# Long attention of a decoder: weighing in bursts of two groups every fourth tick, with 12 exponential buffers, remainders and jobs moved beside the bursts

## The chip, the cores and the metric

The kernel runs on one core of one Trainium2 chip, as one launch. The metric is the time of the whole launch on the device, in microseconds; lower is better. Work inside the core is split over engines with queues of their own: TensorE (PE), whose weight loads are listed apart as PEld, VectorE (DVE), ScalarE (ACT), GpSimd (POOL) and SyncE (SP), which here issues transfers. They meet at semaphores alone.

## The reference

A decoder of four layers over 8 batches of 100 tokens with 128 features, with three different blocks in each layer. Eleven of the twelve blocks are untouched by the change. The one that is touched is the eleventh, cross attention of the tokens to a context of 1444 rows with 16 query heads of 8 features and 4 key heads:

```python
# B=8, query length 100, key length 1444, H=16, HK=4, HD=8, G=4
q = (query @ Wq).reshape(b, qlen, H, HD)
k = (key @ Wk).reshape(b, kvlen, HK, HD)
v = (value @ Wv).reshape(b, kvlen, HK, HD)
scores = einsum('bqkgd,bskd->bkgqs', q.reshape(b, qlen, HK, G, HD), k) / sqrt(HD)
attn = softmax(scores, axis=-1)
out = einsum('bkgqs,bskd->bqkgd', attn, v).reshape(b, qlen, H * HD)
return out @ Wo
```

The kernel computes it together with the twelfth block (a small network with binarised weights) in `attention_long`, the last stage of the launch.

## The kernel before

`attention_long` works through batches `b` and, in each, two pairs of heads `p`. A unit `u = 2*b + p` is one pair of heads of one batch. The softmax needs the largest score of each row first, so every score is computed twice. In the first pass `max_scores` (L770) multiplies 128 query rows by 361 keys and VectorE takes the negated maximum straight from PSUM (`maximum`, L521); the rows of the fourth part of the queries are few, and four products of another tile shape, "remainders" (L764, read by L516), take care of them. `combine` (VectorE), `split` (GpSimd), the job NT (`turn_maxima`, L780 and L782 on TensorE), `maxima` (the NB copy on ScalarE, L692) and `add_maxima` (GpSimd, L465) then bring the maxima as extra rows into the queries. In the second pass `score` (L793) computes 128 keys by 400 columns, ScalarE turns them to exponentials (`exps`, L679) into one of `EB` buffers of the tile `E`, and `weigh` (L810) multiplies them by the values into `pO`. A group is two key tiles; `weigh(u, g)` issues its four products, in float32, each in a column group of 32 of the array, so that the four run side by side. The profile has two records for each float32 product, thus eight for a group.

The order on each engine is written out by ticks `t`; a batch begins every `PER` = 26 ticks. A tick with offset `o = t - 26*b` holds on TensorE: two `max_scores`, alternating with two `score`s where a unit is in its second pass, then the jobs of the tick, then a weighing if `group_step(t)` names one. Unit `u` has its 12 score steps from tick `start(u)` on: `26*b + 20` for even units, 13 ticks later for odd ones. So of 26 ticks 24 have two scores each, and offsets 6 and 19 have none. In the kernel before a group is weighed at every second tick, from the third step after `start(u)` on, at offsets 23, 25, 1, 3, 5, 7 and 10, 12, 14, 16, 18, 20. Remainders take the place of `max_scores` at offsets 12 and 13 (`REM_AT`).

Five jobs go with a batch: NT twice, TM (`token_major`, eight small float32 products, L820), TURN (`turn`, L827) and PROJ (`project`, L831). Jobs and scores write to PSUM banks that `banks_in_turn` deals out from estimates in ticks: in the steady part there are three, each given to the item that asks when it has been free longest. A score holds its bank until its exponential has been taken, a job until its reader has read it, and `bank_read` makes TensorE wait for exactly that. From tick `start(15)` on five banks are dealt; from tick 208 (`DRAIN`), when there are no more `max_scores`, jobs have a bank of their own. The four banks `pM` of the first pass wait for VectorE.

ScalarE's order in a tick is: the tick's two exponentials, then `out_copied`, then `maxima` (one tick after NT) or `outT` (one tick after TURN). The first `score` of a unit waits for `add_maxima` of that unit.

Of the kernel before, what the change touches and what calls it, by code (L numbers as in the profile page):

```python
# [14 lines left out]
B, T, D = 8, 100, 128  # L15
# [6 lines left out]
NKT = KT_FULL + 1  # L22
# [213 lines left out]
def attention_long(nc, m, name, wo, out):  # L236
# [3 lines left out]
    PER = 26  # L240
    REM_AT = 12
    S_AT = 20
    NU = 2 * B
    EB = 8

    KEY0 = [CW * (k % 4) + 128 * (k // 4) for k in range(NKT)]
    NT0_AT, NT1_AT, TM_AT, TURN_AT, PROJ_AT = 16, 28, 48, 56, 60
    LAST = PER * (B - 1) + PROJ_AT + 1
    SIGNS_AT = (10, 15)
    DRAIN = PER * B  # L250
# [3 lines left out]
    with ExitStack() as ctx:  # L254
# [3 lines left out]
        QT = s.sb("QT", [128, 3, TOK], BF16)  # L258
        E = s.sb("E", [128, EB, NG * T])
        XQ = s.sb("XQ", [128, TOK])  # L260
# [45 lines left out]
        def start(u):  # L306
            return PER * (u // 2) + S_AT + 13 * (u % 2)

        def unit_step(t):

            for u in range(NU):
                if 0 <= t - start(u) < NKT:
                    return u, t - start(u)
            return None

        def group_step(t):

            for u in range(NU):
                r = t - start(u) - 3
                if 0 <= r < NKT and r % 2 == 0:  # L320
                    return u, r // 2
            return None

# [55 lines left out]
        def score_bank(n):  # L379
            return bank_of["score", n]  # L380

        def key_rows(ap, a):
            return ap[64 * a:64 * a + 64]

        with nc.Block() as block:
# [244 lines left out]
            def _(act):  # L630
# [40 lines left out]
                def exps(u, k):  # L671
                    for a in range(2):
                        n = 24 * u + 2 * k + a
                        act.wait_ge(s_s, n + 1)
                        if n >= EB:
                            v, kk = (n - EB) // 24, (n - EB) % 24 // 2
                            act.wait_ge(s_pv, 4 * (6 * v + kk // 2 + 1))
                        r = NW[k]
                        nc.scalar.activation(E[0:r, n % EB, :], score_bank(n)[0:r, 0:NG * T], ACT.Exp,  # L679
                                             scale=SCALE8).then_inc(s_e, 1)  # L680
# [44 lines left out]
            def _(pe):  # L725
                def bank_read(item):
                    holder = earlier_in_bank[item]
                    if holder is not None and holder[0] == "score":
                        pe.wait_ge(s_e, holder[1] + 1)
                    elif holder is not None:  # L730
                        pe.wait_ge(s_read, number[holder] + 1)
# [19 lines left out]
                def max_scores(n):  # L751
                    b, o = n // (2 * PER), n % (2 * PER)
                    if o == 0:
                        if b >= KB:
                            pe.wait_ge(s_ks, 32 * (b - KB + 1))
                        pe.wait_ge(s_qs, 32 * (b + 1))
                    if n >= 4:
                        pe.wait_ge(s_mr, n - 3)
                    if o // 2 in (REM_AT, REM_AT + 1):
                        if o == 2 * REM_AT:  # L760
                            pe.wait_ge(s_qr, b + 1)
                        c = o - 2 * REM_AT
                        for p in range(2):
                            nc.tensor.matmul(pM[32 * p:32 * p + 32, n % 4, 0:CW], QR[:, p, b, :],  # L764
                                             KS[:, b % KB, c, p, :], start=True, stop=True,
                                             skip_group_check=True).then_inc(s_m, 1)
                    else:
                        p, i = (0, o // 2) if o < 2 * REM_AT else (1, o // 2 - REM_AT - 2)
                        x, c, a = i // NC4, i % NC4, 1 - o % 2
                        nc.tensor.matmul(pM[:, n % 4, 0:CW], key_rows(QS, a)[:, b, p, 128 * x:128 * x + 128],  # L770
                                         key_rows(KS, a)[:, b % KB, c, p, :],
                                         start=True, stop=True).then_inc(s_m, 1)

                def turn_maxima(u):
                    pP = fill(("NT", u))
                    pe.wait_ge(s_mx, u + 1)
                    if u == 0:
                        pe.wait_ge(s_rs, 1)
                    for x in range(3):
                        nc.tensor.matmul(pP[:, 128 * x:128 * x + 128], MXP[:, u % 2, x, :], m.ident16[:, :],  # L780
                                         start=(x == 0), stop=True, skip_group_check=True)
                    nc.tensor.matmul(pP[:, 384:NG * T], MXP[0:64, u % 2, 3, :], RS[:, :], start=False, stop=True,  # L782
                                     skip_group_check=True).then_inc(s_fill, 1)

                def score(u, k, a):
                    b, p = u // 2, u % 2
                    n = 24 * u + 2 * k + a
                    if k == 0:
                        pe.wait_ge(s_add, u + 1)
                    bank_read(("score", n))  # L790
                    if n >= 24 * (NU - 1):
                        pe.wait_ge(s_mr, 2 * DRAIN)
                    nc.tensor.matmul(score_bank(n)[0:NW[k], 0:NG * T],  # L793
                                     key_rows(KS, a)[:, b % KB, k % 4, p, 128 * (k // 4):128 * (k // 4) + NW[k]],
                                     key_rows(QS, a)[:, b, p, :],
                                     start=True, stop=True).then_inc(s_s, 1)

                def weigh(u, g):
                    b, p = u // 2, u % 2
                    pe.wait_ge(s_e, 24 * u + 4 * g + 4)  # L800
                    if u == 0 and g == 0:
                        pe.wait_ge(s_ws, 2)
                    if g == 0 and p == 0 and b >= 1:
                        pe.wait_ge(s_oc, b)
                    for x in range(2):
                        k = 2 * g + x
                        for a in range(2):
                            n = 24 * u + 2 * k + a
                            r = 32 * (2 * x + a)
                            nc.tensor.matmul(pO[r:r + 32, 0:NG * T], V[0:NW[k], b, k, a, 16 * p:16 * p + 32],  # L810
                                             E[0:NW[k], n % EB, :], start=(p == 0 and g == 0),
                                             stop=(p == 1 and g == 5), skip_group_check=True).then_inc(s_pv, 1)
# [12 lines left out]
                def turn(b):  # L825
                    pP = fill(("TURN", b))
                    nc.tensor.transpose(pP[:, 144:144 + T], ON[:, :], m.ident[0:T, 0:T]).then_inc(s_fill, 1)  # L827
# [50 lines left out]

                for t in range(LAST + 1):
                    at_step = unit_step(t)  # L880
                    for a in range(2):
                        if t < PER * B:
                            max_scores(2 * t + a)
                        if at_step is not None:
                            score(*at_step, a)
                    for b in range(B):
                        o = t - PER * b
                        if o == NT0_AT:
                            turn_maxima(2 * b)
                        if o == NT1_AT:  # L890
                            turn_maxima(2 * b + 1)
                        if o == TM_AT:
                            token_major(b)
                        if o == TURN_AT:
                            turn(b)
                        if o == PROJ_AT:
                            project(b)
                    at_group = group_step(t)
                    if at_group is not None:
                        weigh(*at_group)  # L900
                    for i in range(2):
                        if t == SIGNS_AT[i]:
                            turn_signs(i)
                        if t == DRAIN + (16, 18)[i]:
                            turn_rows(i)
                    if t == start(NU - 1) + 13:
                        up(0)
                    if t == PER * (B - 1) + TM_AT + 2:
                        up(1)
                        down(0)  # L910
                    if t == PER * (B - 1) + TURN_AT:
                        up(2)
# [15 lines left out]
def attention_short(nc, m, name, wq, wk, wv, wo, spare, keys="self", bias=None, beside=None):  # L928
# [3 lines left out]
    KD = VH * HD  # L932
    EB = 4
    N = 2 * B
# [2903 lines left out]
def decoder(nc, a, out):  # L3838

    with ExitStack() as ctx:  # L3840
# [112 lines left out]
        if 10 in n:  # L3953
            attention_delta_rule(nc, m)
        held["L3a"].close()
        attention_long(nc, m, "L3x", w["x3o"][:, :], out)


# [197 lines left out]
```

## Time and profile before

| | us |
|---|---|
| median of 3 runs (1068.70, 1074.39, 1077.85) | 1074.39 |
| profiled execution | 1076.63 |
| its span from first to last instruction | 1074.8 |

The profiled execution is 2.2 us above the median, and 1.8 us of it lie outside the span. The long attention begins at about 800 us; its first pass starts at 809 us, its first score at 829 us, its last score at 1051.7 us, and the rest up to 1074.8 us is the end of the last batch and of the twelfth block. Views used below: the page, busy time by stretches, groups of instructions by line, waits, and the timeline. In the timeline a row is a run of equal instructions on an engine: start, time from the first start to the last end, engine, line, operation, output and inputs, shape, count, and in brackets the idle time before it with what ended it. The records of TensorE overlap: their length holds the way through the array too, so that the distance between starts, not the length, says how long the engine was taken.

### The profile page before, as it was taken

The numbers are of one execution on the slowest core, as the hardware profiler recorded it, in microseconds if no ns is written. First come the engines' busy times: TensorE is split into PE (matmuls) and PEld (weight loads), VectorE is DVE, ScalarE is ACT, GpSimd is POOL, SyncE is SP. The second block draws the span as 40 slices with busy tenths as digits, with TensorE's granted clock in tenths as the row PEclk, the third lists the DMA queues.
The fourth block names the chain that finished last, engine by engine and source line by source line (L and its number), as shares of the span: only waits on it lengthen the run. The fifth ranks groups of instructions, "written<-read, shape, count | busy, mean of one in ns | idle before, by whom it ended". The sixth has DMA issues, their size and how long they took to land. (4 is left out here: it accounts for less than half of the span.)

```text
span 1074.8 us, 18594 instructions
## 1 busy us (share of the span) xinstructions
PE 907.2 (84%) x6319; PEld 555.0 (52%) x6328; DVE 740.8 (69%) x2034; ACT 583.3 (54%) x1772; POOL 241.7 (22%) x357
## 2 busy tenths in 40 slices
PE   7998999999797372599679799795768999999997
PEld 4447999998464130345453386492662233333333
DVE  7658777877574798475776555514658888888853
ACT  5885777777323100343535344641443777777784
POOL 5013555554200122233030000341401111111110
PEclk8999999999999685699766999996885999999999
DMA  9610000000003600000001001650212101111000
GB/s 234 156 25 2 2 1 2 2 2 1 1 1 45 78 1 15 16 1 2 0 26 31 1 1 56 180 152 17 43 27 64 25 14 18 27 28 22 2 2 16
DMA packets 76186, 35.85 MB, mean 33 GB/s; under 512 B 35236, under 2 KB 74571, under 8 KB 76092
## 3 DMA queue, kind: packets, MB, share of 16 engines
q1 hardware_dynamic: 73724, 33.61, 13.9%
q8 instruction: 51, 0.84, 0.3%
q0 software_dynamic: 896, 0.63, 0.2%
q10 hardware_dynamic: 1472, 0.41, 0.2%
q14 instruction: 43, 0.35, 0.1%
HBM read 24.42 MB, written 11.05 MB: 33 GB/s over the span
## 5 line engine op out<-in xcount | busy, mean ns | idle before, releaser
L679 ACT ACTIVATE L3x_E<-L3x_pS 128x400 f32<-128x400 f32 (+1 forms) x374 | 163.9, 509 | 48.2 <-PE L3x_pS L793 46.7
L521 DVE TENSOR_REDUCE L3x_NMP<-L3x_pM 128x1 f32<-128x361 f32 x384 | 176.0, 524 | 18.5 <-PE L3x_pM L770 17.5
L793 PE MATMUL L3x_pS<-ctx_tm 64*128 64x400 bf16 (+1 forms) x374 | 102.8, 347 | 5.7 <-ACT L3x_E L679 2.6
L1911 ACT ACTIVATE L0x_E<-L0x_E,ctx_r 128x100 f32<-128x100 f32 x288 | 105.1, 369 | 0.5 <-DVE L0x_E L1791 0.5
L770 PE MATMUL L3x_pM<-ctx_tm 64*128 64x361 bf16 x384 | 97.3, 336 | 3.3 <-DVE L3x_NMP L521 2.4
L810 PE MATMUL L3x_pO<-L3x_E,CT 128*32 128x400 f32 (+1 forms) x768 | 84.8, 514 | 0.6 <-ACT L3x_E L679 0.4
L770 PEld LDWEIGHTS L3x_pM<-ctx_tm 64*128 64x128 bf16 x384 | 29.3, 100 | 79.3 <-DVE L3x_NMP L521 62.6
L1720 POOL TENSOR_TENSOR L0x_E<-L0x_E,L0x_RZ 128x1200 f32<-128x1200 f32 x24 | 52.6, 2192 | 72.4 <-DVE L0x_RZ L1816 72.4
L2037 PE MATMUL L0x_pU<-ctx_tm,L0x_E 128*100 128x129 f32 x576 | 67.8, 273 | 1.1 <-POOL L0x_E L1720 1.1
L2025 PE MATMUL L0x_pS<-L0x_QS,CT 128*128 128x100 f32 x576 | 68.4, 275 | 0.0
L2025 PEld LDWEIGHTS L0x_pS<-L0x_QS,CT 128*128 128x128 f32 x576 | 66.2, 192 | 0.4 <-ACT L0x_QS L1903 0.4
L2037 PEld LDWEIGHTS L0x_pU<-ctx_tm,L0x_E 128*100 128x100 f32 x576 | 64.7, 166 | 2.3 <-POOL L0x_E L1720 1.9
L1911 ACT ACTIVATION_READ_ACCUMULATOR L0x_E<-L0x_E,ctx_r 128x1 f32 x288 | 54.9, 191 | 0.0
L793 PEld LDWEIGHTS L3x_pS<-ctx_tm 64*128 64x128 bf16 (+1 forms) x374 | 30.9, 104 | 46.3 <-ACT L3x_E L679 39.7
L2563 PE MATMUL L1a_pA<-CT,ident 128*128 128x512 f32 (+1 forms) x48 | 24.8, 680 | 27.3 <-DVE CT L2432 27.3
L2416 POOL TENSOR_TENSOR L1a_W<-CT,L1a_KV 128x1280 f32<-128x1280 f32 x5 | 16.1, 3220 | 125.7 <-ACT L1a_KV L2513 87.7
L1784 DVE TENSOR_REDUCE L0x_mx<-L0x_pS 128x4 f32<-128x400 f32 x72 | 40.8, 569 | 2.7 <-PE L0x_pS L2025 1.0
L1791 DVE TENSOR_TENSOR L0x_E<-L0x_pS,L0x_mx 128x400 f32<-128x400 f32 x72 | 38.8, 566 | 0.1
L455 POOL TENSOR_SCALAR L3x_MXP<-L3x_nmx 128x8 bf16<-128x8 f32 x16 | 4.2, 261 | 144.6 <-DVE L3x_nmx L534 144.6
L3053 POOL DMA_INDIRECT slots_in<-L2f_XE,L2f_slot_index x8 | 8.8, 1097 | 119.1 <-issue 119.1
L137 ACT ACTIVATE root<-veps 100x8 f32<-100x8 f32 (+1 forms) x11 | 2.3, 210 | 60.9 <-DVE veps L120 37.7
L2563 PEld LDWEIGHTS L1a_pA<-CT,ident 128*128 128x128 f32 x48 | 11.3, 243 | 40.7 <-issue 34.1
(727 smaller groups left out, 2134.4 us busy)
## 6 DMA issues: line engine op xcount, KB each, us to landing
ctx_tm<-in_ctx SPq DMA_DIRECT2D x8, 704.0 KB
ctx_tm<-key_terms SPq DMA_DIRECT2D x16, 270.8 KB, 4.2
key_terms<-ctx_tm SPq DMA_DIRECT2D x42, 90.2 KB
ctx_tm<-in_L_ffn_wi SPq DMA_DIRECT2D x4, 512.0 KB, 7.5
ctx_tm<-in_L_ffn_wo SPq DMA_DIRECT2D x4, 512.0 KB, 7.8
ctx_tm<-query_terms SPq DMA_DIRECT2D x16, 75.0 KB, 3.3
slots_in<-L2a_zeros SPq DMA_DIRECT2D x8, 129.0 KB
L2f_XS<-slots_in SPq DMA_DIRECT2D x4, 258.0 KB, 3.1
```

The lines of the kernel that those rows point to most:

```text
L521: nc.vector.tensor_reduce(NMP[:, p, i // NC4, a, i % NC4:i % NC4 + 1], v, AX.X, ALU.max, negate=True).then_inc(s_mr, 1)
L679: nc.scalar.activation(E[0:r, n % EB, :], score_bank(n)[0:r, 0:NG * T], ACT.Exp, scale=SCALE8).then_inc(s_e, 1)
L770: nc.tensor.matmul(pM[:, n % 4, 0:CW], key_rows(QS, a)[:, b, p, 128 * x:128 * x + 128], key_rows(KS, a)[:, b % KB, c, p, :], start=True, s ...
L793: nc.tensor.matmul(score_bank(n)[0:NW[k], 0:NG * T], key_rows(KS, a)[:, b % KB, k % 4, p, 128 * (k // 4):128 * (k // 4) + NW[k]], key_rows ...
L810: nc.tensor.matmul(pO[r:r + 32, 0:NG * T], V[0:NW[k], b, k, a, 16 * p:16 * p + 32], E[0:NW[k], n % EB, :], start=(p == 0 and g == 0), stop ...
L1720: nc.gpsimd.tensor_tensor(E[:, n % 3, :, :], E[:, n % 3, :, :], RZ[:, n % 2, :].unsqueeze(2).broadcast_to((128, 12, T)), ALU.mult).then_in ...
L1784: nc.vector.tensor_reduce(mx[:, n % 2, 4 * c:4 * c + 4], pS[:, g % SB, 0:4 * T].rearrange("p (k t) -> p k t", t=T), AX.X, ALU.max).then_in ...
L1791: nc.vector.tensor_tensor(E[:, n % 3, 4 * c:4 * c + 4, :], pS[:, g % SB, 0:4 * T].rearrange("p (k t) -> p k t", t=T), mx[:, n % 2, 4 * c:4 ...
L1911: last = nc.scalar.activation(E[:, n % 3, k, :], E[:, n % 3, k, :], ACT.Exp, scale=m.ctx_r[:, n % B, k:k + 1], accum_out=Z[:, n % 2, k:k + 1])
L2025: last = nc.tensor.matmul(pS[:, g % SB, k * T:(k + 1) * T], m.CT[:, n % B, c:c + 128], QS[:, n % 2, :], start=True, stop=True)
L2037: last = nc.tensor.matmul(pU[0:T, 0:D + 1], E[:, n % 3, k, :], m.ctx_tm[:, n % B, k, :], start=(k == 0), stop=(k == NKT - 1))
L2563: last = nc.tensor.matmul(pC[n % 2][:, c:c + x], m.ident[:, :], P[:, n % 2, c:c + x], start=(i == 0), stop=True, skip_group_check=True)
```

## The change

The buffers for exponentials grow from 8 to 12. `group_step` names every fourth tick, from the fifth step after `start(u)` on, and two groups are weighed there one after the other: bursts at offsets 25, 3, 7 and 12, 16, 20, with sixteen records each. At offset 12 the two remainders are issued behind the tick's scores, just ahead of the burst, and at offset 13 ahead of the scores, just behind the burst. NT1 moves from offset 2 to 3, TM from 22 to 25, TURN from 4 to 1, and PROJ from 8 to 7; NT0 stays at 16. The readers of the jobs on the other engines move along, each one tick behind its job, because they are placed by the same constants. The products, their number and their shapes are the same.

```diff
@@ -241,10 +241,10 @@
     REM_AT = 12
     S_AT = 20
     NU = 2 * B
-    EB = 8
+    EB = 12
 
     KEY0 = [CW * (k % 4) + 128 * (k // 4) for k in range(NKT)]
-    NT0_AT, NT1_AT, TM_AT, TURN_AT, PROJ_AT = 16, 28, 48, 56, 60
+    NT0_AT, NT1_AT, TM_AT, TURN_AT, PROJ_AT = 16, 29, 51, 53, 59
@@ -316,8 +316,8 @@
         def group_step(t):
 
             for u in range(NU):
-                r = t - start(u) - 3
-                if 0 <= r < NKT and r % 2 == 0:
+                r = t - start(u) - 5
+                if 0 <= r < NKT and r % 4 == 0:
                     return u, r // 2
             return None
 
@@ -878,11 +878,18 @@
 
                 for t in range(LAST + 1):
                     at_step = unit_step(t)
+                    remainder = t % PER - REM_AT if t < PER * B else None
+                    if remainder == 1:
+                        max_scores(2 * t)
+                        max_scores(2 * t + 1)
                     for a in range(2):
-                        if t < PER * B:
+                        if t < PER * B and remainder not in (0, 1):
                             max_scores(2 * t + a)
                         if at_step is not None:
                             score(*at_step, a)
+                    if remainder == 0:
+                        max_scores(2 * t)
+                        max_scores(2 * t + 1)
                     for b in range(B):
                         o = t - PER * b
                         if o == NT0_AT:
@@ -897,7 +904,9 @@
                             project(b)
                     at_group = group_step(t)
                     if at_group is not None:
-                        weigh(*at_group)
+                        u, g = at_group
+                        weigh(u, g)
+                        weigh(u, g + 1)
```

## Rows read from the trace of the kernel before

**Rows 1.** The page: granted TensorE clock in 40 slices of the span, in tenths.
```profile
PEclk8999999999999685699766999996885999999999
```

**Rows 2.** Busy time of each engine (instructions) in one period of 26 ticks.
```profile
894.60:923.40 28.80, 27.82 (x223) 9.25 (x219) 25.48 (x64) 22.23 (x53) 4.05 (x12) 1.00 0.16 26
```

**Rows 3.** Groups by line in that period: busy us, mean ns, idle before.
```profile
L521 DVE TENSOR_REDUCE L3x_NMP<-L3x_pM 128x1 f32<-128x361 f32 x50 | 23.1, 525 | 2.6 <-PE L3x_pM L770 2.5
L679 ACT ACTIVATE L3x_E<-L3x_pS 128x400 f32<-128x400 f32 (+1 forms) x49 | 21.6, 506 | 6.4 <-PE L3x_pS L793 6.2
...
L810 PE MATMUL L3x_pO<-L3x_E,CT 128*32 128x400 f32 (+1 forms) x100 | 11.1, 511 | 0.0
```

**Rows 4.** Waits in that period: who for whom, us, times, longest.
```profile
ACT L3x_E L679 <- PE L3x_pS L793: 6.2, 12, 0.9
PEld L3x_pS L793 <- ACT L3x_E L679: 5.0, 14, 0.7
```

**Rows 5.** Timeline of two ticks without a job, offsets 24 and 25.
```profile
919.58 0.49 PE L793 MATMUL L3x_pS<-ctx_tm 64*128 64x400 bf16 x2
...
919.98 1.69 ACT L679 ACTIVATE L3x_E<-L3x_pS 128x400 f32<-128x400 f32 x4 [0.34 <-PE L3x_pS L793]
...
920.53 0.34 PE L793 MATMUL L3x_pS<-ctx_tm 64*128 64x400 bf16 x1
...
920.81 0.88 PE L810 MATMUL L3x_pO<-L3x_E,CT 128*32 128x400 f32 x8
...
921.62 0.32 PE L770 MATMUL L3x_pM<-ctx_tm 64*128 64x361 bf16 x1
...
922.01 1.69 ACT L679 ACTIVATE L3x_E<-L3x_pS 128x400 f32<-128x400 f32 x4 [0.34 <-PE L3x_pS L793]
```

**Rows 6.** Timeline: weighings at offsets 3, 7, 12, 16, 20, then 3; a remainder behind one.
```profile
896.51 0.88 PE L810 MATMUL L3x_pO<-L3x_E,CT 128*32 128x400 f32 x8
...
900.37 0.88 PE L810 MATMUL L3x_pO<-L3x_E,CT 105*32 105x400 f32 x8
...
906.05 0.88 PE L810 MATMUL L3x_pO<-L3x_E,CT 128*32 128x400 f32 x8
906.75 0.33 PE L764 MATMUL L3x_pM<-ctx_tm 128*32 128x361 bf16 x2
...
910.80 0.88 PE L810 MATMUL L3x_pO<-L3x_E,CT 128*32 128x400 f32 x8
...
914.80 0.88 PE L810 MATMUL L3x_pO<-L3x_E,CT 105*32 105x400 f32 x8
...
925.31 0.88 PE L810 MATMUL L3x_pO<-L3x_E,CT 128*32 128x400 f32 x8
```

**Rows 7.** Timeline behind the weighing of offset 7, with PROJ: two banks for scores.
```profile
901.61 0.46 PE L831 MATMUL L3x_pS<-w_x3o,L3x_OT 128*100 128x128 f32 x2
...
902.14 0.34 PE L793 MATMUL L3x_pS<-ctx_tm 64*128 64x400 bf16 x1
...
903.07 0.34 PE L793 MATMUL L3x_pS<-ctx_tm 64*128 64x400 bf16 x1
```

**Rows 8.** Timeline from NT0 (offset 16) to the first score of the unit.
```profile
910.43 0.33 PE L780 MATMUL L3x_pS<-ident,L3x_MXP 128*128 128x128 bf16 x3
...
912.80 0.49 ACT L692 CAST L3x_NB<-L3x_pS 128x400 bf16<-128x400 f32 x1
...
913.37 0.94 POOL L465 TENSOR_TENSOR ctx_tm<-ctx_tm,L3x_NB 128x400 bf16<-128x400 bf16 x1 [3.34 <-ACT L3x_NB L692]
...
914.37 0.43 PE L793 MATMUL L3x_pS<-ctx_tm 64*128 64x400 bf16 x2
```

**Rows 9.** Timeline behind the weighing of offset 20: exponentials, TM, the next product.
```profile
916.21 1.70 ACT L679 ACTIVATE L3x_E<-L3x_pS 128x400 f32<-128x400 f32 x4
...
917.22 1.19 PE L820 MATMUL L3x_pS<-L3x_selP,L3x_OC 128*100 128x144 f32 x8
918.34 0.33 PE L770 MATMUL L3x_pM<-ctx_tm 64*128 64x361 bf16 x1
```

## The prediction

> **What bounds the kernel now.** I read the page first: from 845 us on TensorE has its full clock, all last slices are nines [rows 1], so a stretch of the long attention can be reckoned in fixed durations. Then the busy time of one period of 26 ticks [rows 2]: of 28.80 us TensorE is busy 27.82, VectorE 25.48, ScalarE 22.23. TensorE looks like the bound, but its records overlap and hold waiting inside the array, so I went on to the waits. ScalarE waits for scores 6.2 us of a period, and TensorE's score loads wait for exponentials 5.0 us [rows 4]. Each waits for the other: a loop, not an engine, sets the pace. The timeline of two ticks shows the loop [rows 5]. Take the first product behind a weighing as time 0 (919.58). The first exponential starts at 0.40. The first three scores have a bank at once; the fourth (920.53, at 0.95) has none before the first exponential is done, 0.56 after that one's start. The weighing starts 0.27 behind that score (920.81), and the next row product 0.81 later (921.62): 0.95 + 0.27 + 0.81 = 2.03 us. ScalarE has run dry meanwhile, 0.34 us. Four exponentials take 1.69 us with one of 0.51 [rows 3, 5], so they follow each other at (1.69 - 0.51) / 3 = 0.39.
>
> **The rule for a stretch.** With three banks score k (k of 4 or more) starts at 0.95 + 0.39 (k - 4). Where a job holds one bank there are two: scores start at 0, 0.17, 0.95, 1.35, 1.90, 2.30, 2.85, 3.25. Rows 7 bear this out: behind the weighing that starts at 900.37 (0 is at 901.18), the third and fifth scores come at 0.96 and 1.89 [rows 6, 7]. VectorE needs 23.1 / 50 = 0.46 a maximum [rows 3]. If its first starts as late as ScalarE's, four banks hold the eighth product until the fourth maximum is taken, 0.40 + 4 x 0.46, about 2.3; that counts only where a stretch has few scores.
>
> **What a burst costs.** Eight records last 0.88 and one 0.51 on average, so the second four start about 0.36 behind the first [rows 3, 5]. Two groups in one burst need two more such passes: 0.81 + 2 x 0.36 = 1.53 us. Bounds: 0.70 more, the distance at which a remainder follows a weighing [rows 6], or a second full 0.81. The saving is real but small. A remainder has the weighing's tile shape and follows at 0.70, a row product at 0.81 [rows 5, 6]: leaving the shape costs 0.11. Two scores take 0.49 and one 0.34, so a score keeps its rows 0.16; entering costs 0.27 less that, 0.11. A pair is worth 0.2 us. Six weighings and about three pairs round the remainders go away in a period: 1.8 us, if nothing else waited.
>
> The Trainium skill, TensorEngine Tiling (Array Packing), Key Properties, says that changing the tiling mode drains the engine; the two prices above agree, and by that rule alone the change would gain (the rival below). Its section PSUM Bottleneck says that tiling hastens TensorE but not the emptying of PSUM, which can become the limit; the three banks of this trace behave so.
>
> What the saving is set against: during 0.27 + 1.53 us of each burst, and 0.40 more until a new score reaches ScalarE, only the scores that three banks hold can be turned, 3 x 0.39 = 1.2 us. Behind it the banks come free one by one at ScalarE's pace, and TensorE cannot work ahead. EB = 12 does not lift this: it holds exponentials, not scores, and it is just what the longer distance to the burst needs. The price of EB itself is nothing.
>
> **The six stretches**, each from the start of one burst to the next; before is read from the starts in [rows 5, 6], after is the 1.53 of the burst, the last score by the rule, 0.27, and what the jobs add.
> - Offsets 25 to 3, before 4.50. Eight scores, but the planner deals one bank to TM (held by estimate for 2.8 ticks from 25), to TURN at 1 and to NT1 at 3, so scores have two: the eighth at 3.25. NT1 then adds 0.25, a change of shape from a score, and 0.37 until the burst [rows 6, 8]: 3.87 + 1.53 = 5.40.
> - 3 to 7, before 3.86. NT1 now lies just ahead of a burst, and its copy NB on ScalarE stands behind the exponentials of offset 4, which come after the burst. Rows 8 show the same at offset 16: from the end of the weighing (911.61) to the first score of the unit (914.37) 2.76 us pass, through two exponentials, NB (0.49) and the addition on POOL (0.94). The unit's first score, the fifth of this stretch, cannot start before 2.76; by the banks it could at 1.9. Before, NB ran under the weighing and this wait wasn't there at offset 7. With the sixth at 2.92 and PROJ (0.46 [rows 7] and a change of shape), about 0.6 until the burst: 3.50 + 1.53 = 5.03.
> - 7 to 12, before 5.68. Ten scores, one bank dealt to PROJ for the first: the tenth at 3.47; two remainders, 0.27 to the first as to a weighing and 0.15 each: 4.04 + 1.53 = 5.57. Residual and statistics on VectorE lie under the burst.
> - 12 to 16, before 4.75. Two remainders first, 0.30, then eight scores, the last at 2.81. NT0 waits for the bank of the sixth exponential, 0.30 + 0.40 + 5 x 0.39 + 0.56, about 3.20; 0.37: 3.57 + 1.53 = 5.10.
> - 16 to 20, before 4.00. Six scores, the fifth at 2.76 by the addition: 2.87 + 0.32 + 1.53 = 4.72. Before, a weighing lay in this very wait and cost nothing. Now it lies in the bursts.
> - 20 to 25, before 6.01. Ten scores, the first exponential 0.2 late by the copy of `pO` (916.21 is 0.60 behind 915.61 [rows 6, 9]): the tenth at 3.50; TM waits for the bank of the eighth exponential until 3.94, its eight products take 0.94 up to the burst (1.12 to a row product [rows 9]): 4.88 + 1.53 = 6.41. VectorE's normalising lies under the burst.
>
> Sum: before 28.80, after 32.23, +3.4 us. From the burst of tick 25 to that of tick 207 there are seven periods: +24.0.
>
> Ends: up to tick 215 the drain has the same two bad stretches without maxima, +0.7 and +1.9. Behind it five banks hold 1.9 us of exponentials against a silence of 1.80 + 0.40: +0.5 for two bursts. Near the end TURN stands ahead of two pieces of the last block that lay under VectorE's normalising: +0.5. The first ticks at half clock I leave at zero. Total +27.6. The profiled execution would go from 1076.6 to 1104; the median lies 2.2 below it, so **1102 us** (1074.4 + 27.6).
>
> **The rivals.**
> 1. The burst starves ScalarE, but the additions and the two-bank stretches are hidden: three-bank times throughout with VectorE's hold at 2.3 give 4.7, 4.4, 5.4, 5.1, 4.1 and 6.2, in all 29.9, +1.1 a period, with the ends about +10: 1084. For it: estimates of the planner are not waits. Against it: rows 7 and 8 show both waits as they stand. Chance 0.14.
> 2. The other side: the switches of shape set the pace, and the bank waits are only where TensorE happens to stand. It decides if scores can be issued less than 0.39 apart on average behind a burst. Then 9 pairs x 0.2 = 1.8 us a period go, 7.5 periods: 1061. For it: TensorE's 27.82 of 28.80 busy [rows 2]. Against it: the fourth score of every stretch waits for an exponential [rows 4, 5]. Chance 0.08.
> 3. Gains and losses cancel, 1070 to 1080: chance 0.06, for sums of many small terms. A second group that costs 0.81 rather than 0.72 adds 48 x 0.09 = 4; a clock that falls because TensorE waits more would add beyond 1112, 0.02.
>
> **How the numbers follow.** The forecast has 0.70, its own range 1092 (additions hidden in half of the cases, passes at 0.34) to 1112 (second group at 0.81, further job waits of 0.6 a period). Rival 1 carries the low end to 1080. Range 1080 to 1113. Taking 1% as what can be told from no change (1063.6 to 1085.1): slower 0.80, the forecast and part of rival 1; same 0.12; faster 0.08.
>
> **What would show it.** In the changed kernel: sixteen L810 records in about 1.6 us; a period of 32.2 us against 28.8; ScalarE's idle before L679 from 6.4 to about 9 us a period; in the stretch behind offset 3 a first score of the unit that waits for L465, 2.8 behind the burst; scores behind the burst of offset 25 in pairs 0.95 apart. A period under 28.8 with scores 0.17 apart would make the prediction wrong at its root; a period near 30 makes only the job terms wrong.

## The result and the profile after

The changed kernel takes 1116.74 us (median of four runs, 1110.68 to 1124.89); the kernel before ran beside it at 1072.26 us. The ratio is 1.0412, with a 95% interval of 1.037 to 1.0455: 4% slower, 44.5 us. The forecast was 1102, slower by 27.6, with a range to 1113. The direction was right, the size was not.

The profiled execution is the slowest of the four, 1124.89 us, with a span of 1123.1; that is 48.3 us more than the span before. Its mean granted clock is 0.893, that of the other three 0.902, so what this trace says of the clock is more than a middle execution has. The page of the changed kernel gives the first hint. This is the granted clock of TensorE in 40 slices, to be laid beside [rows 1]:

```profile
PEclk8998999999996875998888999969769888879999
```

Before, the last nine slices are all nines. Here four eights and a seven stand in a row in the middle of the long attention. The next fence is the timeline of the changed kernel, weighings alone: start and length of four bursts of sixteen records.

```profile
1017.02 1.55 PE L810 MATMUL L3x_pO<-L3x_E,CT 128*32 128x400 f32 x16
...
1022.08 1.55 PE L810 MATMUL L3x_pO<-L3x_E,CT 105*32 105x400 f32 x16
...
1032.70 1.55 PE L810 MATMUL L3x_pO<-L3x_E,CT 128*32 128x400 f32 x16
...
1037.36 1.55 PE L810 MATMUL L3x_pO<-L3x_E,CT 105*32 105x400 f32 x16
```

They stand at offsets 3, 7, 16 and 20; the burst of offset 12 starts at 1027.34. A burst of two groups lasts 1.55 us from first start to last end, against 0.88 for one group [rows 6]. From 1022.08 to 1032.70, over offsets 7 to 16, 10.62 us pass where 10.43 passed before [rows 6]; the two stretches on either side, 5.06 and 4.66, took 3.86 and 4.00. From earlier in the timeline of the changed kernel come the burst of offset 20, the job TM, the burst of offset 25 and two rows of the scores behind it:

```profile
894.60 1.55 PE L810 MATMUL L3x_pO<-L3x_E,CT 105*32 105x400 f32 x16
900.07 1.20 PE L820 MATMUL L3x_pS<-L3x_selP,L3x_OC 128*100 128x144 f32 x8
901.20 1.55 PE L810 MATMUL L3x_pO<-L3x_E,CT 128*32 128x400 f32 x16
...
902.68 0.49 PE L793 MATMUL L3x_pS<-ctx_tm 64*128 64x400 bf16 x2
...
903.63 0.34 PE L793 MATMUL L3x_pS<-ctx_tm 64*128 64x400 bf16 x1 [0.31 <-ACT L3x_E L679]
```

Offsets 20 to 25 take 6.60 (6.01 before). Offsets 25 to 3 take 5.42 (937.06 to 942.48; 4.50 before). Put together from such stretches, a period at full clock is 32.37 us against 28.80. What seven periods take in this trace, 245.6 us from the burst of tick 25 (832.34) to that of tick 207 (1077.94), is more than seven periods at full clock. These would be about 31.23 + 6 x 32.37 = 225.4: the first of the seven is shorter than the others, 31.23 in a kernel with the same order of products that has it whole at full clock (the one with maxima over 64 columns, below). The rest, 20.2 us, is clock.

The busy times of each engine in short stretches of the changed kernel (us, busy and instructions for PE, PEld, DVE, ACT, POOL, then the granted clock, the share of the DMA engines and GB/s) show what one such place looks like:

```profile
872.50:875.90 3.40, 2.47 (x20) 0.98 (x16) 3.02 (x7) 2.32 (x6) 1.19 (x2) 1.00 0.00 0
875.90:879.30 3.40, 3.40 (x20) 0.77 (x21) 0.79 (x3) 0.65 (x2) 0.00 (x0) 0.50 0.00 0
...
927.10:930.50 3.40, 2.48 (x20) 0.83 (x21) 3.40 (x8) 2.75 (x7) 0.94 (x1) 1.00 0.27 74
930.50:933.90 3.40, 3.40 (x23) 0.89 (x15) 1.51 (x5) 1.89 (x6) 0.00 (x0) 0.51 1.01 134
```

In the first row of each pair TensorE is busy 2.5 of 3.4 us and has the full 2.4 GHz; in the row behind it it is busy throughout and has 1.2 GHz. Each slow row holds a burst or a part of one. Both quiet rows lie in a stretch in which the first score of a unit waits for the addition on GpSimd.

Such rows stand ahead of only half of the falls. Of the twelve half-clock stretches of this trace between 846 and 1048 us, one of 10.2 us and eleven of 3.4, six come behind 3.4 us with 2.47 to 2.52 busy; the other six come behind 2.94 to 3.09, in stretches without a wait for the addition. And TensorE can be less busy than in these and keep its clock. The same view at such a fall, and at a stretch with less work and no fall:

```profile
903.20:906.60 3.40, 3.05 (x17) 1.18 (x16) 3.40 (x8) 3.29 (x9) 0.00 (x0) 1.00 0.00 0
906.60:910.00 3.40, 3.40 (x21) 0.93 (x21) 0.20 (x2) 0.24 (x1) 0.00 (x0) 0.51 0.03 5
...
893.00:896.40 3.40, 2.80 (x27) 0.91 (x26) 2.40 (x6) 1.91 (x6) 0.94 (x1) 1.00 0.63 126
896.40:899.80 3.40, 3.06 (x20) 0.85 (x14) 3.35 (x8) 3.40 (x10) 0.00 (x0) 1.00 0.73 82
```

The timeline of the changed kernel for the first quiet row, at 872.50:

```profile
871.03 1.55 PE L810 MATMUL L3x_pO<-L3x_E,CT 128*32 128x400 f32 x16
872.52 0.32 PE L770 MATMUL L3x_pM<-ctx_tm 64*128 64x361 bf16 x1
872.52 0.49 PE L793 MATMUL L3x_pS<-ctx_tm 64*105 64x400 bf16 x2
...
872.92 0.90 ACT L679 ACTIVATE L3x_E<-L3x_pS 105x400 f32<-105x400 f32 x2 [1.67 <-PE L3x_pS L793]
873.48 0.37 PE L793 MATMUL L3x_pS<-ctx_tm 64*105 64x400 bf16 x1 [0.32 <-ACT L3x_E L679]
...
873.71 0.50 ACT L692 CAST L3x_NB<-L3x_pS 128x400 bf16<-128x400 f32 x1
...
874.28 0.94 POOL L465 TENSOR_TENSOR ctx_tm<-ctx_tm,L3x_NB 128x400 bf16<-128x400 bf16 x1 [7.09 <-ACT L3x_NB L692]
...
875.28 0.43 PE L793 MATMUL L3x_pS<-ctx_tm 64*128 64x400 bf16 x2 [0.60 <-POOL ctx_tm L465]
...
876.20 0.89 PE L810 MATMUL L3x_pO<-L3x_E,CT 105*32 105x400 f32 x4
```

The row product (L770) is 1.49 behind the start of the burst. ScalarE had been idle 1.67 us when its first exponential came. The first score of the odd unit (875.28) comes 2.76 behind the end of the burst (872.52, where the next product starts), exactly as at offset 16 before [rows 8], and TensorE had waited 0.60 for L465.

### The profile page after: what moved, and what is told of

Same layout as the page of the kernel before. It is cut to its first block and busy times, and to the rows that moved or that the text cites. A ratio compares the mean times of both kernels' runs of the same rounds, so it can differ in the third digit from the quotient of the medians.

```text
span 1123.1 us, 18599 instructions
## 1 busy us (share of the span) xinstructions
PE 933.7 (83%) x6328; PEld 569.9 (51%) x6328; DVE 735.8 (66%) x2034; ACT 578.4 (52%) x1772; POOL 244.2 (22%) x357
## 5 line engine op out<-in xcount | busy, mean ns | idle before, releaser
L679 ACT ACTIVATE L3x_E<-L3x_pS 128x400 f32<-128x400 f32 (+1 forms) x374 | 160.3, 524 | 96.1 <-PE L3x_pS L793 95.2
L793 PE MATMUL L3x_pS<-ctx_tm 64*128 64x400 bf16 (+1 forms) x374 | 115.1, 366 | 22.8 <-ACT L3x_E L679 12.6
L770 PE MATMUL L3x_pM<-ctx_tm 64*128 64x361 bf16 x384 | 109.5, 349 | 2.5 <-DVE L3x_NMP L521 2.0
L810 PE MATMUL L3x_pO<-L3x_E,CT 128*32 128x400 f32 (+1 forms) x768 | 93.5, 598 | 0.1
L770 PEld LDWEIGHTS L3x_pM<-ctx_tm 64*128 64x128 bf16 x384 | 34.9, 105 | 56.4 <-DVE L3x_NMP L521 27.8
L2425 POOL TENSOR_TENSOR L1a_W<-CT,L1a_KV 128x1280 f32<-128x1280 f32 x5 | 18.7, 3737 | 124.6 <-ACT L1a_KV L2522 88.4
L1793 DVE TENSOR_REDUCE L0x_mx<-L0x_pS 128x4 f32<-128x400 f32 x72 | 40.8, 568 | 2.9 <-PE L0x_pS L2034 1.2
L810 PEld LDWEIGHTS L3x_pO<-L3x_E,CT 128*32 128x32 f32 (+1 forms) x768 | 25.2, 122 | 32.2 <-issue 21.8
L465 POOL TENSOR_TENSOR ctx_tm<-ctx_tm,L3x_NB 128x400 bf16<-128x400 bf16 x16 | 15.0, 938 | 91.1 <-ACT L3x_NB L692 91.1
```

Of the source, the lines that this page charges most:

```text
L793: nc.tensor.matmul(score_bank(n)[0:NW[k], 0:NG * T], key_rows(KS, a)[:, b % KB, k % 4, p, 128 * (k // 4):128 * (k // 4) + NW[k]], key_rows ...
L1793: nc.vector.tensor_reduce(mx[:, n % 2, 4 * c:4 * c + 4], pS[:, g % SB, 0:4 * T].rearrange("p (k t) -> p k t", t=T), AX.X, ALU.max).then_in ...
```

## The experiments

Theory A, of the prediction: a burst outlasts what three score banks hold, and the moved jobs put new waits into the loop of TensorE and ScalarE. Theory B, formed from the trace after: on top of that TensorE then has too little to do, its clock falls to the lower level for some microseconds, and bursts run at half speed (the busy time of single rows alone cannot show it, as the rows above say; the runs have to). Rivals: the jobs alone carry the loss; the banks are not what counts; the clock falls for the long float32 bursts themselves.

**Bursts alone.** The kernel before with this and nothing else:

```diff
-    EB = 8
+    EB = 12
-                r = t - start(u) - 3
-                if 0 <= r < NKT and r % 2 == 0:
+                r = t - start(u) - 5
+                if 0 <= r < NKT and r % 4 == 0:
-                        weigh(*at_group)
+                        u, g = at_group
+                        weigh(u, g)
+                        weigh(u, g + 1)
```

> The bursts of two groups every fourth tick and the 12 buffers alone; the jobs and the remainders stay where they are in the kernel before. Theory of the prediction (three score banks run dry under a burst of 1.5 us, whatever stands beside it): a period of about 31.3 us at full clock against 28.8, thus 1090 to 1095, and more if the TensorE clock falls as it does in the changed kernel. Rival (the loss is in the moved jobs, NT1's copy above all, and the burst itself is harmless): a period within 0.5 us of 28.8, 1070 to 1077.

Measured: 1090.75 us, ratio 1.014 (1.0114 to 1.0166). The period is 30.72 us, read from the starts of bursts 26 ticks apart (894.71, 925.42, 956.14). The clock is whole, as the busy times of one period show:

```profile
925.40:956.10 30.70, 28.54 (x220) 10.37 (x219) 25.38 (x63) 21.87 (x53) 4.04 (x11) 1.00 0.15 24
```

Theory A holds in kind, 1.9 us a period where 2.5 were expected, although this kernel has the 12 buffers. The rival of the harmless burst falls.

**Moved jobs and remainders alone.** The changed kernel with `EB = 8`, offset 3 and `r % 2` in `group_step`, and one `weigh` for a call.

> The moved jobs and remainders alone, with single groups at every second tick and 8 buffers. Theory: the shape changes round the remainders go (0.6 us a period), NT1 ahead of a weighing makes the unit's first score wait for the addition on GpSimd (0.2 to 0.5 a period): 1069 to 1076, and the clock stays whole. Rival (the moved jobs carry the loss): 1085 or more.

Measured: 1093.38 us, ratio 1.0167 (1.0136 to 1.0199), a period of 30.50. This was a miss, and the rival named with it was right: they cost 1.70 us a period, nearly as much as the bursts. The timeline shows one reason. TM stands right ahead of the weighing now, so ScalarE gets nothing for the length of both, and is idle 1.64 us; TM at its old place left it idle 0.83.

```profile
892.12 1.20 PE L820 MATMUL L3x_pS<-L3x_selP,L3x_OC 128*100 128x144 f32 x8
...
893.25 0.88 PE L810 MATMUL L3x_pO<-L3x_E,CT 128*32 128x400 f32 x8
...
894.46 1.84 ACT L679 ACTIVATE L3x_E<-L3x_pS 128x400 f32<-128x400 f32 x4 [1.64 <-PE L3x_pS L793]
...
895.01 0.34 PE L793 MATMUL L3x_pS<-ctx_tm 64*128 64x400 bf16 x1 [0.31 <-ACT L3x_E L679]
```

The last row is the third score behind the weighing, 0.95 behind its first: two banks, because the third is dealt to TM, then to TURN.

**Which part of these.** Three kernels, each the one before with one part. Remainders:

> The kernel before with only the new places of the remainders: behind the scores of offset 12, ahead of those of offset 13, next to the single weighing of offset 12. The run with moved jobs and remainders had a period of 30.50 against 28.80, with 0.65 less from offset 7 to 12 and 0.42 more from 12 to 16. Theory (the remainders give back shape changes, the loss there is the jobs' alone): a period of 28.2 to 28.8, 1070 to 1075. Rival (the remainders ahead of offset 13 delay scores and maxima and carry a part of the 1.7): a period of 29.0 or more, 1077 or more.

Measured: 1073.36 us, ratio 0.9983 (0.9963 to 1.0003). The period is 28.98, 0.18 more. That lies between what the theory (up to 28.8) and the rival (29.0 or more) expected. From offset 7 to 12 0.25 us are saved, from 12 to 16 0.42 are lost. The time cannot be told from that before.

TM alone, `TM_AT` 48 to 51:

> The kernel before with TM alone moved, from offset 22 to 25 (TURN, NT1 and PROJ as before). The moved jobs and remainders cost 1.7 us a period together, the remainders 0.2 of it. Theory (TM and the weighing right behind it are one silence of two microseconds for ScalarE, and TM's bank is dealt away for the ticks behind it): 0.8 to 1.2 a period, 29.6 to 30.0, 1081 to 1086. Rival (TM only changes places with as much waiting, the loss is with NT1, TURN and PROJ): 29.1 or less, up to 1077.

Measured: 1078.78 us, ratio 1.0062 (1.0033 to 1.009), a period of 29.55, 0.75 more: both just under the theory's range, the time above the rival's. Of it 0.35 lie between offsets 20 and 25 (3.04 + 3.33 against 3.97 + 2.04) and 0.40 in the next stretch.

NT1, TURN and PROJ, `NT1_AT` 28 to 29, `TURN_AT` 56 to 53, `PROJ_AT` 60 to 59:

> The kernel before with NT1, TURN and PROJ at their new places and TM and the remainders where they were. Theory (TM carries the most): 0.2 to 0.6 a period more, 29.0 to 29.4, 1074 to 1080. Rival (NT1's late copy and the shortened chain carry the loss): 29.8 or more, 1082 or more.

Measured: 1080.54 us, ratio 1.0082 (1.0053 to 1.0112), a period of 29.75, 0.95 more, above the theory's 0.2 to 0.6 and next to the rival's 29.8. So TM does not carry the most. The three parts add to 1.88 where the kernel with all of them has 1.70. With the bursts: 1.92 + 1.70 = 3.62, and the changed kernel at full clock has 3.57 more than before. The losses simply add.

**One job back.** The changed kernel with `NT1_AT = 28`.

> The changed kernel with NT1 one tick earlier (28, as before), so that its copy on ScalarE stands ahead of the burst of offset 3 and runs beneath it. Theory: the first score of the odd unit no longer waits for the addition on GpSimd; the stretch from offset 3 to 7 goes from 5.06 to 4.2 to 4.4 us, 0.7 to 0.9 a period, about 6 us less than the changed kernel, give or take what the clock does. Rival (that wait lies beside VectorE's hold on the last maxima and is worth nothing): no difference to the changed kernel beyond its spread.

Measured: 1109.32 us, ratio 1.0324 (1.0288 to 1.036). The stretch from offset 3 to 7 is 4.50 in place of 5.06; the one ahead of it takes 5.61 instead of 5.42, so at full clock a period is 31.98, 0.38 less. That is 2.7 us over seven periods. The ratios differ by 0.0088, 9.4 us, with intervals that just part; the other 7 may lie with the clock, as this trace has four half-clock stretches of 3.4 us in its periods in place of twelve. It is not shown that the earlier NT1 is the reason: the number changes from kernel to kernel without it too (the next run has five with the order of the changed kernel). The wait is real, and about half of what it was thought to be worth.

**A fourth bank for scores.** First the ground, the changed kernel with maxima over 64 of the 361 columns, which leaves a part of the maxima out:

```diff
-                    v = pM[:, n % 4, 0:CW]
+                    v = pM[:, n % 4, 0:64]
```

> The changed kernel with each maximum taken over 64 of the 361 columns of its product (a part of the maxima is left out), so that VectorE cannot hold the banks of the first pass; the ground for the next run. Both theories: little change, 32.0 to 32.4 a period where the clock is whole, as the banks of the scores and not VectorE set the pace; if VectorE's maxima set it, 31 or less.

Measured: 1106.84 us (two runs, ratio 1.0304, 1.0255 to 1.0353), and 32.36 a period at full clock, the same as with full maxima, although VectorE falls to 12.08 us busy of 32.40. VectorE does not set the pace of the changed kernel. The median is all the same 9.9 us lower. This trace has five half-clock stretches of 3.4 us in its first three periods and then four whole periods without one, with the same products in the same order: when the clock falls is not settled by the order alone. The waits of one of the whole periods, to be laid beside [rows 4], show the loop at the new pace:

```profile
PEld L3x_pS L793 <- ACT L3x_E L679: 10.5, 28, 0.7
ACT L3x_E L679 <- PE L3x_pS L793: 9.8, 7, 2.3
```

TensorE's score loads wait 10.5 us of a period for exponentials where they waited 5.0. Then the bank (shortened):

```diff
-        shared = [pS[:, 0, :], pS[:, 1, :], pS[:, 2, :], pM[:, 1, :], pM[:, 2, :]]
+        shared = [pS[:, 0, :], pS[:, 1, :], pS[:, 2, :], pM[:, 3, :], pM[:, 1, :], pM[:, 2, :]]
-                usable = 5 if t >= start(NU - 1) else 3
+                usable = (0, 1, 2, 4, 5) if t >= start(NU - 1) else (0, 1, 2) if t >= DRAIN else (0, 1, 2, 3)
-                    if n >= 4:
-                        pe.wait_ge(s_mr, n - 3)
+                    if n >= 3:
+                        pe.wait_ge(s_mr, n - 2)
```

and `n % 3` in place of `n % 4` for the first pass's banks.

> As the run with maxima over 64 columns, but with three banks for the first pass and four instead of three dealt to scores and jobs. Theory (three banks hold too few scores for a burst): the last score ahead of a burst comes 0.39 earlier where no job holds a bank and 0.74 earlier where one does, nothing where the addition on GpSimd is awaited: 1.9 us a period less than the run with three banks, 30.2 to 30.6 at full clock, 14 us or more in all. Rival (banks are only where TensorE happens to stand, the order of products sets the pace): within 3 us of the run with three banks.

Measured: 1088.44 us (two runs), 18.4 less, and a period of 30.62, 1.74 less; 1.9 were expected. Seven periods of it make 12.2 of the 18.4. The busy times of one period, first with three banks for scores, then with four:

```profile
963.60:996.00 32.40, 28.72 (x224) 10.43 (x223) 12.08 (x62) 21.53 (x52) 4.09 (x12) 1.00 0.10 18
```

```profile
950.80:981.40 30.60, 27.65 (x220) 10.58 (x219) 11.87 (x62) 21.23 (x53) 4.03 (x12) 1.00 0.10 20
```

The same products in the same order, one bank more for scores: the banks are what a burst runs out of. The clock falls here too, three times in the seven periods, for 3.4 us each. The stretches that wait for the addition kept their 5.06 and 4.67.

**The same for the kernel before**, with all of the work:

> The kernel before with three banks for the first pass and four dealt to scores and jobs, all of the work done. With maxima over few columns a fourth bank was worth 1.74 us a period of the changed kernel. Theory: single weighings leave silences of 0.27 + 0.81 + 0.43, 1.5 us, which three banks of maxima (1.3 us of VectorE's work) just do not cover, so that VectorE, 25.5 of 28.8 busy, takes 0.2 more per weighing while scores gain: 28.3 to 29.0 a period, 1068 to 1076. Rival (score banks are what bounds the kernel before too, and VectorE has room): 28.0 or less, 1066 or less.

Measured: 1072.14 us, ratio 0.9995 (0.9971 to 1.0018), a period of 28.50, 0.30 less. What the scores gain the maxima lose: the stretches from offset 5 to 7 and 18 to 20 go from 1.39 and 1.53 to 2.12, three with a job from 2.47 to 2.08, and in a period the loads of the row products wait 11.2 us for maxima where they waited 6.7. No version that beats the kernel before came out of this.

**The clock, held.** The changed kernel with more streaming where TensorE waits for ScalarE:

```diff
+                        t = n // 2
+                        if t > start(0) and unit_step(t) is not None and group_step(t - 1) is None:
+                            nc.tensor.matmul(pM[:, n % 4, 0:CW], key_rows(QS, a)[:, b, p, 128 * x:128 * x + 128],
+                                             key_rows(KS, a)[:, b % KB, c, p, :], start=True, stop=True)
```

> The changed kernel with each product of the first pass issued twice into the same bank (the second overwrites the first with the same numbers) in ticks with scores that are not the first behind a burst: more streaming on TensorE where it waits for ScalarE. Theory (the half-clock stretches of the changed kernel come from TensorE having too little to do behind and between bursts): no half-clock stretch between 860 us and the end of the second pass, a period of 32.4 to 33 us throughout, 1100 to 1106. Rival (the clock falls for the long float32 bursts themselves, or by chance of the run): half-clock stretches stay, 1116 or more.

Measured: 1108.01 us, ratio 1.0304 (1.0276 to 1.0333), below the interval of the changed kernel (1.037 to 1.0455) with 34 products more in a period, and above the 1100 to 1106 that were expected. The busy times of two periods:

```profile
894.40:927.20 32.80, 30.68 (x258) 13.23 (x261) 25.44 (x63) 21.53 (x52) 4.07 (x11) 1.00 0.14 23
927.20:960.00 32.80, 30.68 (x258) 13.22 (x261) 25.43 (x63) 21.53 (x52) 4.07 (x11) 1.00 0.14 23
```

Every period from 861 to 1058 us is 32.78, at full clock. Behind them, in the drain, where there are no products of the first pass left to double, one half-clock stretch of 10.2 us comes at 1068 us: there the expectation missed. The extra products cost 0.41 a period, the clock gave back more. The mean granted clock of the whole launch agrees in every execution and not only in the profiled one: 0.912 to 0.915 in the four of this run, 0.893 to 0.902 in the four of the changed kernel. The same bursts are in it, so they do not make the clock fall by themselves.

**The clock, lost without bursts.** The kernel before with two banks for scores and jobs (`usable = 5 if t >= start(NU - 1) else 2`), one look:

> The kernel before with two instead of three banks dealt to scores and jobs. By the rule for two banks a pair of ticks without a job takes 2.43 instead of 2.03 us, and where a job holds a bank scores come 0.95 apart: a period of 33 to 36 us. If the clock falls because TensorE has little to do (and not for long float32 bursts, of which this kernel has none), half-clock stretches come in the second pass here too; if it falls for the bursts, none.

Measured: 1139.28 us in a single run, periods of 37.4 to 40.8 behind the first, longer than the 33 to 36 expected: where a job holds one of two banks only one is left. Two pairs of stretches:

```profile
892.90:896.30 3.40, 2.52 (x24) 0.70 (x16) 2.04 (x4) 2.15 (x5) 0.77 (x1) 1.00 0.00 0
896.30:899.70 3.40, 3.40 (x24) 0.62 (x18) 1.86 (x4) 1.08 (x4) 0.17 (x1) 0.50 0.83 152
930.40:933.80 3.40, 2.52 (x20) 0.70 (x16) 1.99 (x4) 2.02 (x5) 0.64 (x1) 1.00 0.02 5
933.80:937.20 3.40, 3.40 (x24) 0.54 (x18) 1.91 (x5) 1.16 (x3) 0.31 (x1) 0.50 0.79 150
```

The same picture as in the changed kernel, without one burst of two groups: 2.5 us busy of 3.4, then half clock. But this trace has the same rows without a fall behind them:

```profile
909.90:913.30 3.40, 2.47 (x24) 0.85 (x20) 1.95 (x4) 2.29 (x5) 0.00 (x0) 1.00 0.02 5
913.30:916.70 3.40, 2.51 (x21) 0.92 (x20) 1.95 (x4) 2.04 (x5) 1.19 (x2) 1.00 0.00 0
```

So theory B stands as far as this: more waits can bring half-clock stretches, without bursts of two groups too, and in the changed kernel products put into the waits took them out of the seven periods. Which wait tips the clock, and when, no run here settles.

## Why the prediction was right in direction and wrong in size

**The loop and the bank rule: right.** At full clock the six stretches came out as follows.

| offsets | before | forecast | measured |
|---|---|---|---|
| 25 to 3 | 4.50 | 5.40 | 5.42 |
| 3 to 7 | 3.86 | 5.03 | 5.06 |
| 7 to 12 | 5.68 | 5.57 | 5.26 |
| 12 to 16 | 4.75 | 5.10 | 5.36 |
| 16 to 20 | 4.00 | 4.72 | 4.67 |
| 20 to 25 | 6.01 | 6.41 | 6.60 |
| period | 28.80 | 32.23 | 32.37 |

Seven periods cost 225.4 - 200.7 = 24.7 us more (before, 835.31 to 1036.01, its first one shorter too), the sum had 24.0. The experiment with the fourth bank confirms the rule itself, 1.74 against 1.9.

**The price of a burst: right within 0.05.** 1.49 from its start to the next row product, 1.53 forecast. The other marks named there are seen too: sixteen records in 1.55 us, the unit's first score 2.76 behind the burst, scores 0.95 apart behind the burst of offset 25 (902.68 and 903.63). ScalarE's idle time before its exponentials was forecast at about 9 us a period; in the whole period of the kernel with maxima over 64 columns, of the same length, the waits for scores alone are 9.8.

**Offsets 7 to 16: two errors that cancel.** Forecast 10.67, measured 10.62, and that is luck: the first part is 0.31 shorter and the second 0.26 longer than forecast. The start of the burst of offset 12 came earlier than reckoned, because part of it did not wait for the remainders (below), and the end did not.

**The rivals.** Rival 1, additions and two-bank stretches hidden, is refuted by the stretches 3 to 7 and 25 to 3. Rival 2, shape changes set the pace, is refuted by the periods of the bursts alone and of the fourth bank; where shape changes alone were saved, round the remainders, the run cannot be told from before. Rival 3, gains and losses cancel, is refuted by the time.

**The step that failed: the clock.** The prediction took the full clock of [rows 1] for given in the changed kernel too ("a stretch of the long attention can be reckoned in fixed durations"), and gave a falling clock a chance of 0.02, although it had itself worked out that TensorE would wait more. What the runs showed in its place is a clock that falls to 1.2 GHz for 3.4 us and more at twelve places of the seven periods (their first 2.6 us are still at the 1.2 GHz of the start). In the profiled execution it is 245.6 - 225.4 = 20.2 us. Over the medians it is less, by an estimate: the kernel with the clock held is 11.6 us faster by the ratios' difference (0.0108 x 1074) and pays 7 x 0.41 = 2.9 for its extra products, about 14.5 us, give or take 6 by the two intervals. With 24.7 for the loop, that leaves some 5 of the 44.5 us for the ends, forecast at 3.6, with the same uncertainty. In the profiled execution the part behind the burst of tick 207 is 6.4 us longer (45.2 against 38.8), with one half-clock stretch in it, and the part ahead of the burst of tick 25 is 3.0 shorter, so this term is not settled closer than a few microseconds.

The Trainium skill, TensorE: Matmul & The Clock Gate, A second HAM failure mode: psum-queue depth-cycling, tells of a kernel in which TensorE idles shortly between groups of products as it cycles through PSUM banks, and in which its clock goes back and forth. This trace agrees in kind: at six of its twelve falls 2.47 to 2.52 us busy of 3.40, then 1.2 GHz. It was the rule to weigh beside the bank rule, and the prediction did not name it.

**What the prediction left unsaid.** It put the loss down to the bursts above all. The runs split it almost evenly, 1.92 for the bursts and 1.70 for jobs and remainders. Neither half has a fall of the clock in its seven periods (the jobs alone have one, for 10.2 us, in the drain). In the seven periods the clock falls only where both are together: the medians of the halves are 16.1 and 18.7 us over that of before (1074.68), in all 34.8, and the whole change has 44.5. That more waiting tips the clock there is argued from the runs above, not shown for this sum.

## What to carry to other kernels

Where two engines pass work through a few PSUM banks, reckon the longest silence of the producer against what the banks hold; grouping work to save changes of shape lengthens that silence, and more buffers behind the consumer (12 in place of 8 here) do not take the loss away. When a sum says that TensorE will wait more, give a fall of its clock a real chance and a price in the range: here 14 to 20 us on top of 25 for the waits, at places that the busy time of the single rows did not tell in advance. A job moved beside a burst also moves its reader behind the burst, and the chain that follows from it.

## What the runs showed of the hardware

- In the changed kernel the clock fell six times behind 3.40 us in which TensorE's records covered 2.47 to 2.52, and six times behind 2.94 to 3.09; in the kernel with two banks it stayed up behind 2.47 and 2.51 (909.90 to 916.70). The share that the records cover does not tell a fall in advance. The slowed rows of the changed kernel read as busy throughout (3.40 of 3.40), so that the busy share of TensorE, 31.0 us of 34 in the changed kernel against 32.9 before, hides it; the granted clock shows it.
- Products of a weighing need not wait for remainders that stand ahead of them in program order. In the changed kernel the earliest two records of the burst of offset 12 start 0.03 us behind the first pair of remainders and ahead of the second, and run beside them. The records do not name their column group; by the code the remainders use the groups at 0 and 32, so these two are taken to be the products for the groups at 64 and 96:

```profile
1027.31 0.33 PE L764 MATMUL L3x_pM<-ctx_tm 128*32 128x361 bf16 x2
1027.34 0.53 PE L810 MATMUL L3x_pO<-L3x_E,CT 128*32 128x400 f32 x2
1027.47 0.32 PE L764 MATMUL L3x_pM<-ctx_tm 128*32 128x361 bf16 x2
```
